# The state loop of a four-sequence-pair selective scan: decays of one unit from summed logarithms, a share of the kept product moved between engines, and a readout gathered over 16 steps

## The reference, cut to what matters

```python
delta = jax.nn.softplus(dt @ W_dt.T + b_dt)
A = -jnp.exp(A_log)
def step(h, inp):
    d_t, u_t, B_t, C_t = inp
    dA = jnp.exp(d_t[..., None] * A)
    dBu = (d_t * u_t)[..., None] * B_t[:, None, :]
    h = dA * h + dBu
    y = jnp.einsum('bdn,bn->bd', h, C_t)
    return (h, y)
```

## Time and profile before

| | us |
|---|---|
| median of 3 executions (lowest, highest) | 1983.76 (1981.63, 1995.86) |
| the profiled execution's own time | 1991.11 |
| its span | 1989.3 |
| state loop, first fill to last readout, inside the span | 468.15 to 1073.22 |

### The profile page before, as it was taken

One profiled execution on the slowest core, in us unless ns is written; L12 is line 12 of the kernel. 1 busy time (PEld: TensorE's weight loads), 2 busy tenths in 40 slices (PEclk: granted clock), 3 DMA queues, 4 the chain that ended last, 5 costly groups with the idle time before them and its releaser, 6 DMA issues.

```text
span 1989.3 us, 22637 instructions
## 1 busy us (share of the span) xinstructions
PE 1734.4 (87%) x8392; PEld 840.6 (42%) x8392; DVE 1122.2 (56%) x1523; ACT 660.5 (33%) x1176; POOL 770.0 (39%) x427
## 2 busy tenths in 40 slices
PE   7888886996999999999998858999821889899998
PEld 4666653551332332332333525444410556654443
DVE  2444443178998999998996233222349464521211
ACT  1333331152554554554553131111312240111121
POOL 1333330205998998998997010000200006000000
PEclk8999997896999999999998768999865879889999
DMA  2111101011000000000000500111063100101110
GB/s 71 33 32 32 32 22 51 0 50 52 12 14 20 10 15 21 11 15 21 10 9 15 219 0 0 32 47 32 0 132 82 32 0 1 43 1 42 43 42 21
DMA packets 34944, 65.51 MB, mean 33 GB/s; under 512 B 12740, under 2 KB 21848, under 8 KB 33188
## 3 DMA queue, kind: packets, MB, share of 16 engines
q1 hardware_dynamic: 34868, 64.49, 11.0%
HBM read 55.80 MB, written 8.67 MB: 32 GB/s over the span
## 4 chain that ended last, share of the span: by engine, by line
PE 51%; POOL 20%; DVE 13%; issue 11%; ACT 2%; DMA 2%; SPq 0%; DVEq 0%; ACTq 0%; POOLq 0%
POOL arena L1006 19%; PE ps L1226 6%; PE ps L1998 6%; PE ps L1987 6%; PE ps L198 4%; PE ps L1239 3%; PE ps L339 3%; PE ps L344 3%; PE ps L221 2%; DVE arena L934 2%; PE ps L357 2%; DVE arena L474 2%; PE ps L1762 2%; PE ps L1778 1%; PE ps L787 1%
## 5 line engine op out<-in xcount | busy, mean ns | idle before, releaser
L1006 POOL TENSOR_TENSOR arena<-arena 128x1024 f32<-128x1024 f32 x248 | 577.8, 2399 | 26.6 <-DVE arena L960 18.2
L787 PE MATMUL ps<-arena 32*128 32x512 f32 x2016 | 473.3, 643 | 24.8 <-DVE arena L941 19.3
L892 ACT ACTIVATE arena<-arena 128x1024 f32<-128x1024 f32 x248 | 262.2, 1057 | 296.7 <-DVE arena L950 296.7
L963 DVE TENSOR_TENSOR arena<-arena,ps 128x1024 f32<-128x1024 f32 x248 | 302.3, 1219 | 9.9 <-POOL arena L1006 8.8
L950 DVE TENSOR_TENSOR arena<-arena,ps 128x1024 f32<-128x1024 f32 x248 | 301.0, 1214 | 10.2 <-PE ps L787 10.2
L787 PEld LDWEIGHTS ps<-arena 32*128 32x128 f32 x2016 | 164.0, 189 | 335.5 <-issue 143.1
L811 PE MATMUL ps<-arena 128*32 128x512 f32 x1024 | 140.4, 621 | 5.2 <-DVE arena L963 3.1
L1226 PE MATMUL ps<-arena 128*128 128x512 f32 x288 | 131.9, 603 | 0.6 <-ACT arena L1291 0.6
L2079 DVE TENSOR_TENSOR arena<-arena,ps 128x512 f32<-128x512 f32 x56 | 38.5, 688 | 160.7 <-ACT arena L2041 160.7
L1944 POOL TENSOR_TENSOR arena<-arena 128x1024 f32<-128x1024 f32 x16 | 29.9, 1895 | 226.6 <-DVE arena L1877 213.3
L1987 PE MATMUL ps<-arena 128*128 128x512 f32 x256 | 116.6, 600 | 0.0
(11 more groups left out here) (275 smaller groups left out, 2221.2 us busy)
## 6 DMA issues: line engine op xcount, KB each, us to landing
arena<-ctxT SPq DMA_DIRECT2D x32, 257.0 KB, 3.1
arena<-ctxT SPq DMA_DIRECT2D x8, 1028.0 KB, 15.4
arena<-L_ffn_w SPq DMA_DIRECT2D x16, 512.0 KB, 4.2
arena<-ctx_rows SPq DMA_DIRECT2D x8, 960.0 KB
m_rows<-arena SPq DMA_DIRECT2D x16, 256.0 KB, 2.6
arena<-m_rows SPq DMA_DIRECT2D x64, 64.0 KB
arena<-L_ffn_eW SPq DMA_DIRECT2D x8, 512.0 KB, 3.6
m_yd<-arena SPq DMA_DIRECT2D x64, 32.0 KB
```

Source lines behind the costliest of these rows:

```text
L787: mm = nc.tensor.matmul(ps[:, ring(n) + jj, :], weights[r], m_row[r, buf, t % CH, :], start=True, stop=True)
L892: nc.scalar.activation(m_xa[:, u, t % 2], m_xa[:, u, t % 2], ACT.Exp, scale=-1.0).then_inc(S["m_dec"], 1)
L963: nc.vector.tensor_tensor(m_h[:, u, t % 2], m_xa[:, u, t % 2], ps[:, ring(n):ring(n) + 2, :], ALU.add).then_inc(S["m_use"], 1)
L1006: nc.gpsimd.tensor_tensor(m_xa[:, u, t % 2], m_xa[:, u, t % 2], m_h[:, u, (t - 1) % 2], ALU.mult).then_inc(S["m_kept"], 1)
```

## The change

- The loop runs over n = 0 to 127 without a break between groups. Rates and decays are made two steps ahead (n+2) instead of one, across the border of a group.
- Unit 0 keeps its way: fill `rates`, `rate` on DVE, one exponential on ACT (`decay`). Of its kept product POOL now does columns 0 to 767 and DVE the last 256 (`carry` in `m_dve`, both inputs in SBUF, and DVE waits for its own result: `ch.link`).
- Unit 1 has no `rate` on DVE any more. SP stores ln(delta) for its rows (ACT's `logged`, semaphore `m_ln`), and `logs` on PE adds, in one pair of banks, A_log (two matmuls of 64 rows, from `m_al`) and ln(delta) (two of 32 rows). ACT takes an exponential out of PSUM (`m_lus`) and a second one of the negative in place: `decay_log`. Its kept product stays on POOL, 1024 columns.
- The order on PE in step n is drive(n, 0), readout of n-1, rates(n+2), drive(n, 1), logs(n+2). The ring of three bank pairs stays (`room`); a bank pair of `logs` comes free with ACT's first exponential.
- The readout of 16 steps stays in one bank: step k writes 2*(16-k) rows of each of the four column groups, so that later steps leave the last two rows of each earlier one. ACT copies the bank once in 16 steps, SP writes it with 8 DMAs, and the later turn uses products with a permutation (`m_back`) in place of transposes.
- Ahead of the loop: `m_id2`, `m_back` on DVE, `m_tiny` on POOL, 8 small products and a copy for `m_al`, four logarithms on ACT.

In the tables of counts, 504 uses become 380 and 128 bank copies become 8:

```diff
-TURNS = [("m_fill", 504, "t_cen"), ("m_use", 504, "t_conv"), ("m_y", 128, "t_gate"), ("m_yev", 128, "t_mask"),
+TURNS = [("m_fill", 504, "t_cen"), ("m_use", 380, "t_conv"), ("m_y", 128, "t_gate"), ("m_yev", 8, "t_mask"),
```

The core of the diff:

```diff
+        YS = 16
+        m_ys = view(30 * K, 2, DI)
         m_yt = view(18 * K, TT, DI)
         m_yg = view(22 * K, IC, T)
-        NY = L // YB
...
+        STEPS = GROUPS * L
+        SHARE = 256
+        def rated(n):
+            return n < STEPS and n % L > 0
+        m_order = [("r", 1), ("l", 1)]
+        for n in range(STEPS):
+            m_order += [("d0", n)] + [("r", n + 2)] * rated(n + 2) + [("d1", n)] + [("l", n + 2)] * rated(n + 2)
+        m_pos = {x: k for k, x in enumerate(m_order)}
+        m_used = {x: k + 1 for k, x in enumerate(x for x in m_order if x[0] != "l")}
+        m_turn = {x[1]: k for k, x in enumerate(x for x in m_order if x[0] == "r")}
...
-                sp.wait_ge(*S.at(("m_delta", "m_dudone")[ty], q + 1))
+                if ty == 0 and q % 2:
+                    sp.wait_ge(*S.at("m_ln", q // 2 + 1))
+                else:
+                    sp.wait_ge(*S.at(("m_delta", "m_dudone")[ty], q + 1))
+                src = m_du if ty else m_p if q % 2 else m_delta
                 sp.dma_start(m_rows[ty, 4 * q:4 * q + 4].rearrange("s t d -> (s t) d"),
-                             (m_delta, m_du)[ty][:, q, :]).then_inc(S[f"m_st{q // 4}"], 16)
+                             src[:, q, :]).then_inc(S[f"m_st{q // 4}"], 16)
...
+                sp.wait_ge(*S.at("m_yev", v + 1))
+                for j in range(GP):
+                    for z in range(SEQS):
+                        sp.dma_start(m_yd[8 * (v // 2) + 2 * j + z, v % 2],
+                                     m_ys[32 * j + z:32 * j + 32:2, v % 2]).then_inc(S[f"m_yk{v % 2}"], 16)
...
+            for c in range(IC):
+                for jj in range(2):
+                    mm = nc.tensor.matmul(ps[NS * jj:NS * jj + NS, 2, c * P:(c + 1) * P], m_a[:, c, :], ident,
+                                          start=True, stop=True)
+            mm.then_inc(S["m_alt"], 1)
...
+            def room(x):
+                k = m_pos[x]
+                if k >= 3:
+                    gone = m_order[k - 3]
+                    if gone[0] == "l":
+                        pe.wait_ge(*S.at("m_lus", m_turn[gone[1]] + 1))
+                    else:
+                        pe.wait_ge(*S.at("m_use", m_used[gone]))
+                return ring(k)
...
+            def spread(bank, weights, n, u, start=True):
                 for jj in range(2):
                     r = slice(32 * (2 * u + jj), 32 * (2 * u + jj) + 32)
-                    mm = nc.tensor.matmul(ps[:, ring(n) + jj, :], weights[r], m_row[r, buf, t % CH, :], start=True, stop=True)
+                    mm = nc.tensor.matmul(ps[:, bank + jj, :], weights[r], m_row[r, n // CH % 2, n % CH, :],
+                                          start=start, stop=True)
...
+            def rates(n):
+                arrived(n)
+                spread(room(("r", n)), sel, n, 0)
+            def logs(n):
+                bank = room(("l", n))
+                for jj in range(2):
+                    r = slice(NS * jj, NS * jj + NS)
+                    nc.tensor.matmul(ps[:, bank + jj, :], m_id2[r].rearrange("p s n -> p (s n)"), m_al[r], start=True, stop=False)
+                spread(bank, sel, n, 1, start=False)
+            def drive(n, u):
+                arrived(n)
+                spread(room((f"d{u}", n)), m_blk[:, n // CH % 2, n % CH].rearrange("p s n -> p (s n)"), n, u)
...
+                v, k = n // YS, n % YS
+                rows = 2 * (YS - k)
+                pe.wait_ge(*S.at("m_use", m_used["d1", n]))
+                if k == 0 and v >= 2:
+                    pe.wait_ge(*S.at("m_yev", v - 1))
                 for u in range(2):
                     for jj in range(2):
                         j = 2 * u + jj
-                        o = ((GP * g + j) * L + t) * SEQS
-                        mm = nc.tensor.matmul(ps[32 * j:32 * j + 32, 6 + n % 2, :], m_C[:, o:o + 32], m_h[:, u, t % 2, jj, :],
-                                              start=True, stop=True)
+                        o = FRONT + ((GP * (n // L) + j) * L + n % L) * SEQS + 2
+                        mm = nc.tensor.matmul(ps[32 * j:32 * j + rows, 6 + v % 2, :], m_C[:, o - rows:o],
+                                              m_h[:, u, n % 2, jj, :], start=True, stop=True)
...
+            rates(1)
+            logs(1)
+            for n in range(STEPS):
+                drive(n, 0)
+                if n:
+                    read_out(n - 1)
+                if rated(n + 2):
+                    rates(n + 2)
+                drive(n, 1)
+                if rated(n + 2):
+                    logs(n + 2)
+            read_out(STEPS - 1)
...
-                        mm = nc.tensor.transpose(ps[:, 4 * h + c, i * P:(i + 1) * P],
-                                                 m_yt[:, 4 * h + i, c * P:(c + 1) * P], ident)
+                        mm = nc.tensor.matmul(ps[:, 4 * h + c, i * P:(i + 1) * P], m_yt[:, 4 * h + i, c * P:(c + 1) * P],
+                                              m_back.rearrange("p a b -> p (a b)"), start=True, stop=True)
...
+            def logged(h):
+                for q in (4 * h + 1, 4 * h + 3):
+                    act.wait_ge(*S.at("m_delta", q + 1))
+                    nc.scalar.activation(m_p[:, q, :], m_delta[:, q, :], ACT.Ln, bias=m_tiny[:, 0:1]).then_inc(S["m_ln"], 1)
+            logged(0)
...
-            def decay(g, t, u):
-                act.wait_ge(*S.at("m_use", fill_x(g, t, u) + 1))
-                nc.scalar.activation(m_xa[:, u, t % 2], m_xa[:, u, t % 2], ACT.Exp, scale=-1.0).then_inc(S["m_dec"], 1)
-            def keep(n):
-                v = n // YB
-                act.wait_ge(*S.at("m_y", n + 1))
-                if v >= 2 and n % YB == 0:
-                    act.wait_ge(*S.at(f"m_yk{v % 2}", 32 * (v // 2)))
-                nc.scalar.copy(m_ys[:, v % 2, n % YB, :], ps[:, 6 + n % 2, :]).then_inc(S["m_yev"], 1)
...
+            def decay(n):
+                act.wait_ge(*S.at("m_use", m_used["r", n]))
+                nc.scalar.activation(m_xa[:, 0, n % 2], m_xa[:, 0, n % 2], ACT.Exp, scale=-1.0).then_inc(S["m_dec"], 1)
+            def decay_log(n):
+                act.wait_ge(*S.at("m_fill", m_pos["l", n] + 1))
+                if n >= 2:
+                    act.wait_ge(*S.at("m_use", m_used["d1", n - 2]))
+                bank = ring(m_pos["l", n])
+                nc.scalar.activation(m_xa[:, 1, n % 2], ps[:, bank:bank + 2, :], ACT.Exp).then_inc(S["m_lus"], 1)
+                act.wait_ge(*S.at("m_lus", m_turn[n] + 1))
+                nc.scalar.activation(m_xa[:, 1, n % 2], m_xa[:, 1, n % 2], ACT.Exp, scale=-1.0).then_inc(S["m_dec"], 1)
+            def keep(v):
+                act.wait_ge(*S.at("m_y", YS * v + YS))
+                if v >= 2:
+                    act.wait_ge(*S.at(f"m_yk{v % 2}", 128 * (v // 2)))
+                nc.scalar.copy(m_ys[:, v % 2], ps[:, 6 + v % 2, :]).then_inc(S["m_yev"], 1)
+            decay(1)
+            decay_log(1)
+            for n in range(STEPS):
+                if rated(n + 2):
+                    decay(n + 2)
+                    decay_log(n + 2)
+                if n % YS == 1 and n > YS:
+                    keep(n // YS - 1)
+            keep(2 * GROUPS - 1)
...
+            def carry(n):
+                own = slice(2 * DI - SHARE, 2 * DI)
+                dve.wait_ge(*S.at("m_dec", 2 * m_turn[n] + 1))
+                dve.wait_ge(*S.at("m_use", m_used["d0", n - 1]))
+                x = flat(m_xa[:, 0, n % 2])[:, own]
+                ch.link(nc.vector.tensor_tensor(x, x, flat(m_h[:, 0, (n - 1) % 2])[:, own], ALU.mult))
...
-            for g in range(GROUPS):
-                for t in range(L):
-                    for u in range(2):
-                        if t < L - 1:
-                            rate(g, t + 1, u)
-                        state(g, t, u)
+            rate(1)
+            for n in range(STEPS):
+                if SHARE and n % L:
+                    carry(n)
+                state(n, 0)
+                if rated(n + 2):
+                    rate(n + 2)
+                state(n, 1)
...
-            def carry(g, t, u):
-                pool.wait_ge(*S.at("m_dec", 2 * ((L - 1) * g + t - 1) + u + 1))
-                pool.wait_ge(*S.at("m_use", fill_hs(g, t - 1, u) + 1))
-                nc.gpsimd.tensor_tensor(m_xa[:, u, t % 2], m_xa[:, u, t % 2], m_h[:, u, (t - 1) % 2],
+            def carry(n, u):
+                own = slice(0, 2 * DI if u else 2 * DI - SHARE)
+                pool.wait_ge(*S.at("m_dec", 2 * m_turn[n] + u + 1))
+                pool.wait_ge(*S.at("m_use", m_used[f"d{u}", n - 1]))
+                x = m_xa[:, u, n % 2].rearrange("p j d -> p (j d)")[:, own]
```

(7 more changed lines are left out.)

154 lines of the change are left out of this document (65 added, 89 removed).

## The result

The changed kernel takes 1980.6 us (median of 19 runs, 1973.2 to 1988.2), the kernel before 1990.4 in as many runs (1981.6 to 2008.5). The ratio is 0.9949, 95% interval 0.9932 to 0.9967: half a per cent or 10 us faster, where 4 us and 1979.5 were forecast. The profiled execution spans 1972.3 us against 1989.3. Of these 17.0 us, 16.9 are the loop (first fill at 464.20 to last readout at 1052.38, 588.2 against 605.1), and -6.0 the tail (from there to the first weight load of the product with W_out, 17.8 against 11.8); 4.0 lie ahead of the loop, 3.6 of them already at 36 us, in layer 0, and 2.1 behind the tail, so those 6.1 are not the change's. -16.9 + 6.0 = -10.9 agrees with the ratio, whose interval means 7 to 13 us.

What follows compares the result with a forecast made beforehand. GpSimd's two products bound the kernel before (4.66 us a step); a new chain of 4.57 would bound. Loop -9 and tail +5 gave about -4 us: 1979.5 from the median 1983.8, range 1966 to 2006.

Steps and rivals of the forecast that it cites:

- The step: Steady loop step: 4.57 us against 4.66 before; 122 intervals at 4.57, four without a rate at about 3.9.
- the chain: Unit 1's state, readout, rates fill, VectorE's rate, next state: each waits for the one before, sum 4.57 us a step.
- The start: Loop start at half clock: 8.7 us to unit 1's first state, 7.6 for the first interval.
- The clock: TensorE clock dips of 7 us behind groups' ends, about 2.8 us each; 5 of the possible 8 us taken.
- 4.13 + x: GpSimd's step sum: products of 2.33 and 1.80 us plus hand-over x with VectorE, taken as 0.18; 4.31, hidden behind 4.57.
- Rivals 1 and 2: GpSimd/VectorE hand-over: 1, dear, x 0.66, step 4.79, 2006 us, chance 0.17; 2, x about 0.53, step 4.66, 1990, 0.11.
- TensorE: PE's work in a step: readout 0.99 and three blocks of about 1.06, sum 4.2 us, below the 4.57.
- rival 3: PE becomes the bound: fills cannot run together or shape changes cost more; 5.2 us a step, 2057 us, chance 0.05.
- rival 4: Readout shrinks with its output rows, GpSimd's 4.31 would bound, loop gains another 32 us: 1948 us, chance 0.07.
- second chain: Unit 1's state, ScalarE's exponential out of PSUM, drive, A_log, ln(delta), next readout: 4.32 us, hidden by 0.25.
- The tail: Behind the last readout: 8 DMA issues add 3.0 us, products for transposes 1.7 to 3.4; 5 taken.
- Ahead of the loop: Logarithms, small products and copies hidden beside DVE's polynomial: nothing added; without that cover some 4 us.

Runs made afterwards that it cites:

- read2: Changed kernel with every readout matmul issued twice: step 5.448 us, 2094 us in its one run.
- narrow: Changed kernel with the readout 32 columns wide instead of 512 in 15 of 16 steps: step 4.367 us, 1952 us in its one run.
- share512: Changed kernel with VectorE taking 512 columns of unit 0's kept product instead of 256: 1984.3 us, ratio 0.9970 to the kernel before, step 4.565.
- direct: Changed kernel with y kept in SBUF and turned from there, without the DMA trip through memory: 1970.9 us, ratio 0.9868 to the kernel before.
- share0: Changed kernel with GpSimd multiplying all 1024 columns of unit 0 again, none on VectorE: 1995.3 us, ratio 1.0019 to the kernel before, step 4.646.
- nolog_xa3: Changed kernel without the logarithms (unit 1's rates on VectorE again), no columns on VectorE, and a third buffer for the rates: step 4.650 us.
- late_noA: Changed kernel with three state buffers, reading out step n-2, and without the A_log matmuls: step 4.493 us, 1993 us.
- late: Changed kernel with a third state buffer, reading out step n-2 instead of n-1: 1978.6 us, ratio 0.9877 to the kernel before, step 4.492.

## Why the prediction was right

The time was within 1.1 us, but the change was put at -4 us and is -10: the median of the three runs from which it was counted (1983.8) lay 6.6 us below that of the 19, and the two offset each other. That the time came so close is luck; that the step did is not, as the runs on its links show. All of the size that was missed lies in the loop (16.9 us gained where 9 were forecast); by the prediction's own steps:

**The step.** Forecast 4.57, measured 4.567, each link within 0.02. `read2` (+0.88) and `narrow` (-0.20, to the ScalarE chain) show that the readout is in the chain, `share512` that GpSimd isn't. The sum of 122 steps at 4.57 and four at 3.9 came as put: four intervals are 3.91 or 3.92, though they lie two steps ahead of a group's last state, not at the border.

**The start.** To the first state of unit 1 8.7 us were taken and 8.66 measured. The first interval was put at 7.6 and took 5.05: the clock was up 7 us after the first fill, where I had a readout at half speed. 2.5 us of the loop.

**The clock.** I took 5 us for dips behind the groups' ends. None came in the profiled execution. That is the term of the sum that was mis-sized, and with the start it is 7.5 of the 7.8 us between the 596 forecast for the loop and the 588.2 measured. Single dips of 3.4 us cost 1.4 to 1.7 us each in `share512` and `direct`, and 1.0 to 1.1 in `share0` and `nolog_xa3`, not 2.8. Already in the kernel before only two of the three lasted 7 us; the one behind the second group, at 775.4, lasted 3.4, which the earlier trace rows doesn't show. `late_noA` has dips of 7 to 27 us, so longer ones do come with the new order. The reason that I gave for them (TensorE idles at a border) isn't shown by any run.

**GpSimd.** The 4.13 + x: 768 columns took 1.82 (1.80 forecast), x was 0.18 in the sum and 0.17 in the steps of `narrow` in which GpSimd never idles, the only ones in which it counts. Rivals 1 and 2 needed 0.44 and more. In the changed kernel VectorE's columns begin first (702.18 against 702.40) and aren't held up: 0.42 us, as forecast.

**TensorE.** Its four blocks are 1.00, 1.18, 1.06 and 1.34 with a wait for the state in the last; I had 4.2 for the sum, and the joined pairs are 0.1 dearer than the 1.06 taken. The pairs do run together, against rival 3. Readouts of 2 and of 32 rows both take 0.59 to 0.61 us a matmul, against rival 4. The second chain that I named, over ScalarE (4.32), is there at 4.37 and sets most steps of `narrow`; but it was not the next one: `late` shows one of 4.49 through the bank of the rates, which the forecast lacked.

**The tail.** Forecast +5 (3.3 to 6.5), measured +6.0. The issues are 0.69 us each, not 0.5, so 4.5 us more instead of 3.0; the products cost 2.0 more, of which I had 1.7 to 3.4.

**Ahead of the loop** nothing was forecast, and of the 4.0 us that the profile gains there 3.6 stood at 36 us, long before the first changed instruction (GpSimd's `m_tiny` at 295.5).
